# Two of eight convolution tiles moved from VectorE to TensorE, and the positive part of softplus issued one unit later, in a state-space mixer

## The reference, cut to what matters

```python
x_inner, z = split(xz)                       # 1024 channels each
xc = silu(causal_conv(x_inner, conv_w) + conv_b)     # 4 taps, each channel by itself
x_ssm = xc @ x_proj_w.T                      # 16 B, 16 C, 1 for dt
dt = softplus(x_ssm[..., -1:] * dt_w + dt_b)
h = exp(dt * A) * h + dt * B_t * u_t         # one step of the scan over tokens
y_t = sum(h * C_t) + D * u_t
out = (y * silu(z)) @ out_proj_w.T + residual
```

## Time and profile before

| | us |
|---|---|
| median of three runs | 2933.59 |
| profiled execution, its own time | 2948.0 |
| its span, first to last instruction | 2946.5 |
| first and last scan of the mixer start at | 503.6 and 1637.5 |
| VectorE busy over the span | 1931.3 |
| TensorE matmuls busy | 2490.5 |
| ScalarE busy | 1419.7 |
| GpSimd busy | 1225.9 |

### The profile page before, as it was taken

The page is one execution under the profiler, slowest core; times in us unless marked ns, Lnnn a source line. Parts: engine busy times, 40 slices in busy tenths (PEclk is TensorE's granted clock), DMA queues, the critical chain, the costliest instruction groups (busy, mean ns, idle before and its releaser), DMA issues. The chain is left out here.

```text
span 2946.5 us, 48652 instructions
## 1 busy us (share of the span) xinstructions
PE 2490.5 (85%) x17204; PEld 2111.1 (72%) x17205; DVE 1931.3 (66%) x2751; ACT 1419.7 (48%) x3477; POOL 1225.9 (42%) x774
## 2 busy tenths in 40 slices
PE   4999996788888888888887781999999589999986
PEld 4999996788788888888886661444444367877775
DVE  7666533999999999999999435222222366777563
ACT  0341426888888888888888220111111123334432
POOL 3200002666666666666667374000000355454331
PEclk9997978999999999999999865999999788899996
DMA  5910000000000000000000054456654221111000
GB/s 200 409 39 1 1 1 30 30 30 31 30 31 30 31 30 31 30 31 30 30 30 30 21 139 158 150 176 224 196 177 144 79 59 43 32 43 32 8 8 15
DMA packets 65817, 209.60 MB, mean 71 GB/s; under 512 B 12730, under 2 KB 17978, under 8 KB 62778
## 3 DMA queue, kind: packets, MB, share of 16 engines
q1 hardware_dynamic: 25210, 96.00, 9.4%
q0 software_dynamic: 28576, 89.16, 9.4%
q10 hardware_dynamic: 11808, 21.50, 1.9%
HBM read 130.00 MB, written 76.62 MB: 70 GB/s over the span
## 5 line engine op out<-in xcount | busy, mean ns | idle before, releaser
L846 POOL TENSOR_TENSOR m_hs<-m_hs,m_BC 128x1040 f32<-128x1040 f32 x256 | 619.0, 2418 | 382.1 <-DVE m_hs L959 382.1
L765 ACT ACTIVATE m_dA<-m_dt,m_A 128x128 f32<-128x128 f32 x2048 | 614.3, 393 | 185.4 <-DVE m_hs L959 110.9
L640 PE MATMUL m_py<-m_hs,ident 128*128 128x130 f32 x4096 | 533.3, 285 | 142.5 <-POOL m_hs L846 142.3
L959 DVE TENSOR_TENSOR_SCAN m_hs<-m_dA,m_own 128x1040 f32<-128x1040 f32 x256 | 593.2, 2317 | 35.5 <-ACT m_dA L765 22.5
L640 PEld LDWEIGHTS m_py<-m_hs,ident 128*128 128x128 f32 x4096 | 500.3, 198 | 161.4 <-POOL m_hs L846 159.0
L944 DVE TENSOR_TENSOR m_own<-m_BC,m_own 128x1040 f32<-128x1040 f32 x256 | 318.7, 1245 | 18.3 <-issue 4.5
L592 PE MATMUL m_pw<-m_xg,m_w_in 128*128 128x130 f32 x2048 | 273.0, 294 | 51.1 <-DVE m_xc L907 34.7
L592 PEld LDWEIGHTS m_pw<-m_xg,m_w_in 128*128 128x128 f32 x2048 | 264.1, 209 | 54.7 <-DVE m_xc L907 37.8
L1436 PE MATMUL e_pG<-e_w_gu,e_xT 128*128 x656 | 233.5, 499 | 11.1 <-issue 7.2
L1416 POOL DMA_DIRECT2D e_x<-regions x80 | 42.9, 536 | 401.7 <-PE e_pX L1427 401.7
L1436 PEld LDWEIGHTS e_pG<-e_w_gu,e_xT 128*128 128x128 f32 x656 | 118.8, 191 | 90.9 <-issue 24.1
(11 more groups left out here) (287 smaller groups left out, 4496.7 us busy)
## 6 DMA issues: line engine op xcount, KB each, us to landing
m_BC<-xs SPq DMA_DIRECT2D x16, 2080.0 KB, 10.0
slots<-a_zero POOLq DMA_DIRECT2D x48, 512.0 KB, 44.2
e_w_gu<-in_gate_up_w SPq DMA_DIRECT2D x32, 768.0 KB
e_x<-regions POOLq DMA_DIRECT2D x82, 256.0 KB, 3.0
slots<-e_y ACTq DMA_DIRECT2D x82, 256.0 KB, 2.5
regions<-a_zero POOLq DMA_DIRECT2D x16, 512.0 KB, 15.6
e_w_d<-in_down_w SPq DMA_DIRECT2D x32, 256.0 KB
out_h<-t_ho SPq DMA_DIRECT2D x8, 520.0 KB
```

The lines of the kernel that those rows point to most:

```text
L640: mm = pe.matmul(py[k % 2][:, 0:MT], ident[:, :], hs[u % NB][:, n, :], start=False, stop=(half == 1 and n == HN - 1))
L765: act.activation(images(dA[u % NB][:, n, :])[:, :, 1:TOK], images(dt[b][:, k, :])[:, :, 1:TOK], ACT.Exp, scale=A[:, at:at + 1]).then_inc(d ...
L846: pool.tensor_tensor(hs[u % NB][:, :, :], hs[u % NB][:, :, :], BC[b][:, ST + half * HN:ST + (half + 1) * HN, :], ALU.mult).then_inc(prod_r ...
L959: dve.tensor_tensor_scan(hs[u % NB][:, :, :].rearrange("p n t -> p (n t)"), dA[u % NB][:, :, :].rearrange("p n t -> p (n t)"), bu, 0.0, AL ...
```

## The change

Three things change. First, `relus` stands after unit 13 instead of unit 12 (`STEP_AT + 2`). Second, tiles 6 and 7 (`PE_TILES`) of each turn but the first are convolved on TensorE: ScalarE copies them out of PSUM into `e1` (one Copy instead of two tap instructions), eight matmuls with diagonal matrices of the tap weights put the sum back into `pw[2]`, and ScalarE's Silu reads it from there with the bias, one instruction for each of the two tiles, beside one for the other six. The third piece of z, which overwrites `pw[2]`, is issued after unit 5 instead of unit 4 and waits for these two Silu instructions (`pw_free`). VectorE's third `conv_piece` is gone, and eight instructions before turn 0 build the diagonals. Third, the buffer `lp` is gone: what it held is kept in `dt[b]` until the Relu instructions overwrite it, which therefore wait for L830 (`log_steps`).

```diff
@@ pe: in_piece, conv, turn @@
                 if side == 1:
-                    pe.wait_ge(conv_ready, q * ET + PIECES[j][-1] + 1)
+                    if j == 2 and not first:
+                        pe.wait_ge(pw_free, q)
+                    else:
+                        pe.wait_ge(conv_ready, dve_tiles(q) + PIECES[j][-1] + 1)
...
+            def conv(q):
+                pe.wait_ge(tap0, (q + 1) * ET)
+                for at in range(len(PE_TILES)):
+                    for s in range(KC):
+                        mm = pe.matmul(images(pw[2][:, at * MT:(at + 1) * MT])[:, :, s:TOK], diag[:, at * KC + s, :],
+                                       images(e1[:, at, :])[:, :, 0:TOK - s], start=(s == 0), stop=(s == KC - 1))
+                mm.then_inc(pe_conv, 1)
...
-                        if GATE_AT <= u < GATE_AT + NP:
+                        if u == PE_CONV_AT:
+                            if first:
+                                pe.wait_ge(diag_set, len(PE_TILES) * KC)
+                            conv(g + 1)
+                        if GATE_AT <= u < GATE_AT + NP - 1:
                             in_piece(g + 1, 1 - b, 1, u - GATE_AT)
+                        if u == GATE_AT + NP:
+                            in_piece(g + 1, 1 - b, 1, NP - 1)
                         if u == XPROJ_AT:
                             x_proj(g + 1, 1 - b)
@@ act: tap_piece, silus, steps, relus, turn @@
+                if j == 2 and not first:
+                    n = len(PE_TILES)
+                    act.activation(e1[:, 0:n, :], pw[j][:, 0:n * MT].rearrange("p (j t) -> p j t", t=MT), ACT.Copy).then_inc(tap0, n)
+                    return
...
-                act.wait_ge(conv_ready, (q + 1) * ET)
-                act.activation(xc[b][:, :, :], xc[b][:, :, :], ACT.Silu).then_inc(u_ready, 1)
+                    act.wait_ge(pe_conv, q)
+                    for at, e in enumerate(PE_TILES):
+                        silu = act.activation(xc[b][:, e, :], pw[2][:, at * MT:(at + 1) * MT], ACT.Silu, bias=conv_b[:, e:e + 1])
+                    silu.then_inc(pw_free, 1)
+                    act.wait_ge(conv_ready, dve_tiles(q) + DT)
+                    act.activation(xc[b][:, 0:DT, :], xc[b][:, 0:DT, :], ACT.Silu).then_inc(u_ready, 1)
...
-                act.activation(lp[:, :, :], e1[:, :, :], ACT.Identity, bias=-1.0).then_inc(ln_steps, 1)
+                act.activation(dt[b][:, :, :], e1[:, :, :], ACT.Identity, bias=-1.0).then_inc(ln_steps, 1)
...
+            def relus(q, b):
+                act.wait_ge(log_steps, q * 2 + 1)
...
-                        if u == STEP_AT + 1:
-                            relus(1 - b)
+                        if u == STEP_AT + 2:
+                            relus(g + 1, 1 - b)
@@ pool: log_step @@
-                    pool.tensor_tensor(ex[:, :, :], ex[:, :, :], lp[:, :, :], ALU.subtract).then_inc(log_steps, 1)
+                    pool.tensor_tensor(ex[:, :, :], ex[:, :, :], dt[b][:, :, :], ALU.subtract).then_inc(log_steps, 1)
@@ dve: turn, prologue @@
-                    elif not last and CONV_AT <= u < CONV_AT + NP:
+                    elif not last and CONV_AT <= u < CONV_AT + NP - 1:
                         conv_piece(g + 1, 1 - b, u - CONV_AT)
...
+            for at, e in enumerate(PE_TILES):
+                for s in range(KC):
+                    dve.tensor_scalar(diag[:, at * KC + s, :], ident[:, :], conv_w[:, e, KC - 1 - s:KC - s], None, ALU.mult).then_inc(diag_set, 1)
```

More of the change, by code:

```diff
@@ L444 @@
 CONV_AT, ADD_AT = 3, 11
+PE_TILES = PIECES[2]
+PE_CONV_AT = 3
 class MambaWeights:
@@ L509, in mamba @@
         e1 = sb("e1", [P, ET, MT])
-        lp = sb("lp", [P, ET, MT])
+        diag = sb("diag", [P, len(PE_TILES) * KC, P])
         xs = sb("xs", [XP, MT])
@@ L532, in mamba, with dve_tiles @@
         y_ready, out_done, h_ready = map(sem, ("y_ready", "out_done", "h_ready"))
+        diag_set, pe_conv, pw_free = map(sem, ("diag_set", "pe_conv", "pw_free"))
+        DT = ET - len(PE_TILES)
+        def dve_tiles(q):
+            return q * DT + len(PE_TILES) if not (isinstance(q, int) and q == 0) else 0
         block = ctx.enter_context(nc.Block())
@@ L705, in root, with tap_piece @@
                 act.activation(scale[:, :, :], scale[:, :, :], ACT.Exp, scale=-0.5).then_inc(scale_ready, 1)
-            def tap_piece(q, b, j):
+            def tap_piece(q, b, j, first=False):
                 act.wait_ge(in_done, q * 2 * NP + j + 1)
+                if j == 2 and not first:
+                    n = len(PE_TILES)
+                    act.activation(e1[:, 0:n, :], pw[j][:, 0:n * MT].rearrange("p (j t) -> p j t", t=MT), ACT.Copy).then_inc(tap0, n)
+                    return
                 for at, e in enumerate(PIECES[j]):
@@ L712, in tap_piece, with silus @@
                                    scale=conv_w[:, e, KC - 1:KC]).then_inc(tap0, 1)
-            def silus(q, b):
-                act.wait_ge(conv_ready, (q + 1) * ET)
-                act.activation(xc[b][:, :, :], xc[b][:, :, :], ACT.Silu).then_inc(u_ready, 1)
+            def silus(q, b, first=False):
+                if first:
+                    act.wait_ge(conv_ready, ET)
+                    act.activation(xc[b][:, :, :], xc[b][:, :, :], ACT.Silu).then_inc(u_ready, 1)
+                else:
+                    act.wait_ge(pe_conv, q)
[4 more added lines that the diff above has]
+                    act.activation(xc[b][:, 0:DT, :], xc[b][:, 0:DT, :], ACT.Silu).then_inc(u_ready, 1)
                 for j in range(NP):
@@ L729, in take_xs, with steps @@
                 act.activation(xs[:, :], pw[0][0:XP, 0:MT], ACT.Copy).then_inc(xs_ready, 1)
-            def steps(q, first=False):
+            def steps(q, b, first=False):
                 act.wait_ge(s_done, q + 1)
@@ L744, in steps @@
                 act.wait_ge(ln_steps, q * 4 + 2)
-                act.activation(lp[:, :, :], e1[:, :, :], ACT.Identity, bias=-1.0).then_inc(ln_steps, 1)
+                act.activation(dt[b][:, :, :], e1[:, :, :], ACT.Identity, bias=-1.0).then_inc(ln_steps, 1)
                 act.activation(e1[:, :, :], e1[:, :, :], ACT.Ln).then_inc(ln_steps, 1)
-            def relus(b):
+            def relus(q, b):
+                act.wait_ge(log_steps, q * 2 + 1)
                 for e in range(ET):
@@ L777, in turn @@
                         if u == STEP_AT:
-                            steps(g + 1)
+                            steps(g + 1, 1 - b)
                             if more:
@@ L791, in _ @@
             for j in range(NP):
-                tap_piece(0, 0, j)
-            silus(0, 0)
+                tap_piece(0, 0, j, first=True)
+            silus(0, 0, first=True)
             square(1)
@@ L797, in _ @@
             root(1)
-            steps(0, first=True)
-            relus(0)
+            steps(0, 0, first=True)
+            relus(0, 0)
             turn(0, 0, first=True)
@@ L900, in conv_piece @@
                 n = len(PIECES[j])
-                done = (q * ET + PIECES[j][0]) * (KC - 2)
+                done = (dve_tiles(q) + PIECES[j][0]) * (KC - 2)
                 for s in range(1, KC):
@@ L969, in turn @@
                     if not last:
-                        if CONV_AT <= u < CONV_AT + NP and half == 0:
+                        if CONV_AT <= u < CONV_AT + NP - 1 and half == 0:
                             conv_piece(g + 1, 1 - b, u - CONV_AT)
```

## The result

The changed kernel takes 2926.78 us (median of 13 runs, 2919.22 to 2932.13) against 2933.24 us (2927.29 to 2936.58) for the kernel before on the same chips. The ratio is 0.9979, with a 95% interval of 0.9971 to 0.9988: about 6 us faster. The forecast was 2926.9.

The account below looks back on a forecast made before the run. VectorE sets the pace, but from unit 5 to unit 12 ScalarE leads. 14 turns at 0.09 + 0.32 us, plus 1.14 in turn 14, less 0.2 in the prologue, give 6.7 us: 2926.9 us, range 2911 to 2940.

Parts of the forecast that it names:

- The third convolution piece: Removed from VectorE: unit 5's scan 1.25 us sooner, but only 0.09 us a turn gained; the rest becomes unit 12's wait.
- z is not late: Rival: ScalarE gets z's third piece in time, unit 12 gains 0.80 instead of 0.09 us; 2916.2 us in all; chance 0.06.
- The eight matmuls: On TensorE, fit in its 2.33 us wait before z's second piece; taken as 0, bound 2.06 us without that cover.
- The bound below nothing: Filling TensorE's gap before z's second piece may remove the 0.50 clock; TensorE would gain time that nothing waits for.
- the prologue's Relu: Before turn 0 the Relu instructions wait for L830: 0 to 0.3 us once, taken as 0.2.
- The later Relu: Unit 13's scan starts 1.05 us sooner; 0.32 us a turn remains after scale_x is held, 1.05 in turn 14.
- the hold: scale_x (VectorE) is slowed beside GpSimd's L834, both reading two SBUF inputs: bounds 0 and 0.73 us a turn, taken as 0.73.
- No hold: Rival: scale_x runs beside L834 at full speed, 14 turns gain 0.73 us more each; 2916.7 us; chance 0.17.
- The step does not happen: Rival: with the Relu later, unit 13's wait only moves to unit 14; about 0.6 us in all, 2933; chance 0.10.
- the slower rival: TensorE's clock falls to 1.2 GHz over unit 5's sums and z's third piece; 1.4 us a turn lost, 2953; chance 0.15.

Follow-up runs that it names:

- conv_only: The changed kernel with the Relu back after unit 12, so only the convolution moved: 2955.46 us against 2951.83 for the kernel before, ratio 1.0009.
- the early Silu: The changed kernel with ScalarE's Silu group after unit 8 and z's third piece issued after unit 3: 2923.52 us against 2951.83 for the kernel before.
- the shortened addition: The changed kernel with GpSimd's addition for the logarithm cut to one tile of eight: 2935.94 us against 2951.83 for the kernel before, ratio 0.9947.
- relu_only: The kernel before with only the eight Relu moved from after unit 12 to after unit 13: 2945.32 us against 2951.83, ratio 0.998.
- conv_twice: The changed kernel with the convolution's eight diagonal matmuls issued twice: 2927.79 us against 2932.42 for the kernel before, ratio 0.9984.
- both: The changed kernel with Silu and z's third piece earlier, and GpSimd's L830 and L834 after units 9 and 10: 2905.0 us against 2932.42 before.
- the pair on one chip: The kernel before and the changed kernel, both unchanged, run once each on one chip: 2952.2 and 2946.69 us.

## Why the prediction was right

**One turn.** The forecast's working and the trace, in us from the first scan of turn 7:

| | predicted | measured |
|---|---|---|
| scan of unit 5 | 24.21 | 24.21 |
| last z instruction starts | 33.16 | 33.10 |
| scan of unit 12 | 53.01 | 52.91 |
| its wait for `dA` | about 1.5 | 1.35 |
| `scale_x` takes | about 1.4 | 1.39 |
| scan of unit 14 | 62.07 | 61.94 |

**The third convolution piece** freed VectorE 1.25 us early, and nearly all of it became the wait at unit 12. The undisturbed turns of conv_only show it by itself (0.2 us a turn), the early Silu shows what ScalarE's chain was worth. The *z is not late* rival is out: ScalarE waits 0.64 us for the piece. The piece starts at 1041.23, when both its conditions have just been met: the two Silu that free its bank end at 1041.18 (1040.55 + 0.63), and the sums of unit 5 have just been issued.

**The eight matmuls** took no time from the path where they stand, as said. The bound below nothing that I kept, a higher clock once the gap is filled, came true on TensorE: z's second piece takes 2.95 us instead of 4.37. Nothing waited for it, as expected. The 0.2 us for the prologue's Relu came too: from the start of L830 to the end of L839 it is 7.78 us before and 7.99 after.

**The later Relu** gave what unit 13 had waited, less the hold. *No hold* is out, by the 1.39 us and by the shortened addition. *The step does not happen* is out by relu_only.

**What was a little off.** A clean turn gains about 0.53 us instead of 0.41 (0.49 to 0.70 in turns 1 to 12), turns 0 and 13 0.69, and turn 14 1.55 instead of 1.14. Over the turns that is 9.5 us. ScalarE's chain was 0.19 us shorter and not 0.09, because z's third piece started 0.1 us earlier than worked out; the rest is spread over smaller steps. The price in the slower rival was a little high: 4.37/24 less 2.06/16 is 0.05 us a record, not 0.06, so 1.7 us for 32 records and 1.3 a turn.

**What the sum lacked.** 3.3 us of this come back in turns 5 and 9, which last 73.24 and 71.83 us instead of 70.9 (2.3 + 0.9). The slower rival is true there in part, from another place than it named. TensorE of the changed kernel at the start of turn 5:

```profile
873.39 1.16 PE L573 MATMUL m_py<-hT,mean_w 128*128 x8 [1.69 <-DVE m_y L965]
876.23 6.62 PE L660 MATMUL m_py<-m_hs,ident 128*128 128x130 f32 x32 [1.45 <-issue]
```

The granted clock from 876 to 882 is 0.50, the 1.2 GHz level. Ahead of the sums TensorE was idle for 1.69 and 1.45 us. VectorE and ScalarE of the same turn, a few us later:

```profile
883.24 0.69 DVE L922 TENSOR_TENSOR m_dev<-hT,m_py 128x520 f32<-128x520 f32 x1 [1.01 <-PE m_py L660]
```

```profile
900.34 0.39 ACT L758 ACTIVATE m_zs<-m_pw 128x260 f32<-128x260 f32 x1 [1.87 <-PE m_pw L603]
```

VectorE waits 1.01 us for these sums (L922), and ScalarE later 1.87 us for z's third piece, where turn 7 has 0.64. I had looked for the low clock over the sums of unit 5, behind the gap that the matmuls fill, and had put it at nothing at the start of a turn. For comparison the same place in turn 7, which is not long, with the clock over it (1.00):

```profile
1017.64 1.16 PE L573 MATMUL m_py<-hT,mean_w 128*128 x8 [1.70 <-issue]
1020.39 3.74 PE L660 MATMUL m_py<-m_hs,ident 128*128 128x130 f32 x32 [1.37 <-issue]
1017.00:1025.00 8.00, 5.99 (x52) 5.91 (x53) 7.97 (x15) 7.21 (x24) 5.47 (x3) 1.00 0.02 4
```

And turn 5 of the kernel before, which is not long either, with the clock over a part of it (0.50):

```profile
871.98 1.75 PE L565 MATMUL m_py<-hT,mean_w 128*128 x8 [2.01 <-issue]
873.96 4.63 PE L640 MATMUL m_py<-m_hs,ident 128*128 128x130 f32 x32
873.00:875.00 2.00, 2.00 (x11) 2.00 (x10) 2.00 (x3) 2.00 (x7) 1.66 (x3) 0.50 0.00 0
```

So neither the low clock there nor the first gap is new. Turns 3, 5, 7, 9 and 11 have a gap of 1.5 to 2.1 us ahead of L565 or L573 in every profile. In the first profile of the kernel before the clock fell behind it in turns 5, 9 and 11, and none of them is longer for it.

New is the second gap, 0.3 to 1.9 us ahead of the sums. None of the three profiles with the convolution on VectorE has it, nor has conv_twice; in every other kernel with the new matmuls all five turns have it. VectorE's pace doesn't open it: relu_only has it in no turn, with undisturbed odd turns of 71.10 us, and conv_only, with the slower 71.24, in all five. Only in kernels with this gap do the 32 records of the sums take 5.5 us or more in some of these turns, and every long turn is one of them. In conv_twice the clock falls in four of the five turns too, but the sums take at most 5.4 us and no turn is longer.

Whether slow sums cost anything depends on when they end. In turns 5, 9 and 11 of `both` they take 6.0 to 6.6 us, end 14.9 to 15.4 us into the turn, and the turn is not longer. Here they end at 16.6 us in turn 9 and at 18.0 in turn 5, which lose 0.9 and 2.3 us. So the long turns came with the convolution on TensorE, and with them this half of the change brings nothing on balance: relu_only has the same time without it. What the second gap is waiting for, and whether it is what makes the low stretch longer, no run isolates; turn 7 has both gaps at full clock. Why turns 5 and 9 in this kernel and four turns in conv_only are hit stays open.

So the forecast of 6.7 us was met by 9.5 less 3.3, one term too small and one left out. The mechanism of the undisturbed turns is shown; the closeness of 2926.9 to 2926.8 is in part luck, the more so as the first scan's lateness, 2.0 us in the pair on one chip, stands in no term either.

## What to carry to other kernels

When two engines take turns in setting the pace, work taken off the one becomes a wait unless the other's chain shrinks at the same time: follow the freed instruction to the next one that both must pass, and place its feeder (here z's third piece) ahead of work that isn't urgent. Where VectorE and GpSimd both read two inputs from SBUF, order them so that the one on the path starts first (0.17 us was enough here), and after every move look for the next instruction that now starts while the other engine's is still running. Measure each half of a change alone: here the one-line half had all of the gain. Compare stage times and not whole spans when two profiles come from different chips.

## What the runs showed of the hardware

- The hold between VectorE and GpSimd goes by who starts first, and falls on the second comer until the other's instruction is over: `scale_x` went from 0.68 to 1.39 us and `step_input` from 0.28 to 1.21, 1.35 and 1.83, and where both rows are shown they end 0.15 to 0.55 us behind GpSimd's; GpSimd's product went from 2.39 to 2.76 and 2.83 beside a VectorE instruction that was there before it. The scans and the products (L983), which read one input from SBUF and one from PSUM, are not held: the product at 1065.76 starts inside GpSimd's of unit 12 and takes 1.24 us as always. The Trainium skill says the same of such a pair (SBUF — State Buffer, SBUF: two separate sides): the port pair is an exclusive lock, whoever starts first has it for the whole instruction, and on VectorE's side it concerns instructions with two SBUF inputs. The traces agree, with one thing to add: the record of a held instruction begins at once and only ends late, so the hold shows as a long duration and not as a wait.
- TensorE's granted clock fell to 0.50 at the start of single turns of equal work. In turns 5, 9 and 11 of the kernel before (first profile) it cost nothing (32 records of sums in 4.63 us instead of 3.74 in turn 5). In turns 5 and 9 of the changed kernel, the same in both its profiles, it lasted longer (6.62 us in turn 5), and the turns took 0.9 to 2.4 us more. TensorE had been idle for 1.6 to 2.1 us shortly before, but so it had at the start of turns that kept the full clock.
- The stages behind the first scan of turn 15 took 1344 to 1348 or 1365 to 1370 us by the chip, at the same work (the changed kernel 1347.4 and 1367.3): three times what this change is worth.
